# A graph network's edge scatter in groups of 8 columns instead of 16, with the last three tiles of layer 0 reordered

## The reference

```
h = relu(layernorm(x)); t1 = h @ W1
msg = t1[src] + (h[src] * h[dst]) @ W2, divided by sqrt(deg[src] * deg[dst])
e = leaky_relu(t1 + segment_sum(msg, dst) + b);  x = x + e / |e|
```

## Time and profile before

| | us |
|---|---|
| median of 3 runs (range) | 2204.69 (2198.97 to 2205.42) |
| the profiled execution | 2204.25 |
| its span, first to last instruction | 2202.4 |
| first and last scatter of GpSimd start at | 62.36, 1239.11 |
| layer 0's steps, first q to the last gather's end | 483.2 to 1313.5 |
| TensorE busy | 1871.7 (85%) |
| GpSimd busy | 1023.4 (46%) |
| mean granted TensorE clock | 0.895 |

### The profile page before, as it was taken

The page is one execution under the profiler, slowest core; times in us unless marked ns, Lnnn a source line. Parts: engine busy times, 40 slices in busy tenths (PEclk is TensorE's granted clock), DMA queues, the critical chain, the costliest instruction groups (busy, mean ns, idle before and its releaser), DMA issues. The chain is left out here.

```text
span 2202.4 us, 23568 instructions
## 1 busy us (share of the span) xinstructions
PE 1871.7 (85%) x7253; PEld 1153.6 (52%) x7253; DVE 1331.8 (60%) x1958; ACT 484.9 (22%) x635; POOL 1023.4 (46%) x1346
## 2 busy tenths in 40 slices
PE   5599768779999999755566699999879999999996
PEld 1178622257777777433345457777753444434442
DVE  6877678844444445422222355565458788878885
ACT  1000200025555555322233334200250000000000
POOL 1688777777888888888888400000005000000000
PEclk9755579889999999977778899999699999999998
DMA  7888860016666677433343441587016555656553
GB/s 269 328 328 328 336 226 9 9 61 240 239 239 239 243 243 254 157 120 120 140 159 131 167 142 63 192 283 242 27 42 171 155 158 167 189 163 179 166 164 102
DMA packets 338855, 395.86 MB, mean 180 GB/s; under 512 B 114026, under 2 KB 319572, under 8 KB 325843
## 3 DMA queue, kind: packets, MB, share of 16 engines
q1 hardware_dynamic: 219872, 307.83, 39.9%
q10 hardware_dynamic: 93110, 86.22, 11.9%
q0 software_dynamic: 25792, 0.87, 1.0%
HBM read 222.33 MB, written 172.51 MB: 179 GB/s over the span
## 5 line engine op out<-in xcount | busy, mean ns | idle before, releaser
L373 POOL DMA_INDIRECT table<-valT,idxT x806 | 815.9, 1012 | 251.5 <-issue 249.9
L1994 PE MATMUL psum<-wgt,big 128*65 128x384 f32 (+3 forms) x1600 | 527.7, 491 | 2.7 <-POOL big L1855 2.7
L1944 DVE SCALAR_TENSOR_TENSOR wgt<-ratio,l3q,fcj 128x768 f32<-128x768 f32 (+2 forms) x400 | 414.1, 1053 | 96.6 <-PE psum L1994 83.5
L1994 PEld LDWEIGHTS psum<-wgt,big 128*65 128x65 f32 x1600 | 219.0, 137 | 302.5 <-issue 296.0
L784 PE MATMUL psum<-hx,region 128*128 128x257 f32 x1250 | 299.2, 387 | 5.5 <-DVEq L572 5.0
L784 PE MATMUL psum<-region,g 128*128 128x512 f32 (+1 forms) x672 | 270.1, 547 | 1.0 <-DVE big L587 1.0
L587 DVE TENSOR_TENSOR big<-big,psum 128x512 f32<-128x512 f32 (+1 forms) x325 | 209.6, 664 | 86.8 <-PE psum L784 86.4
L784 PEld LDWEIGHTS psum<-hx,region 128*128 128x128 f32 x1250 | 233.6, 195 | 36.5 <-DVEq L572 5.4
L852 PE MATMUL psum<-ident,tk 128*128 128x128 f32 x625 | 104.8, 304 | 151.2 <-DMA tk<-table 150.7
L991 POOL PARTITION_ALL_REDUCE edges<-edge x1 | 0.5, 516 | 396.7 <-DVEq L1363 396.7
L784 PEld LDWEIGHTS psum<-region,g 128*128 128x128 f32 x672 | 121.9, 190 | 118.9 <-issue 112.8
(11 more groups left out here) (215 smaller groups left out, 1487.9 us busy)
## 6 DMA issues: line engine op xcount, KB each, us to landing
table<-tk SPq DMA_DIRECT2D x25, 3200.0 KB
fcj<-counts SPq DMA_DIRECT2D x150, 384.0 KB, 3.3
tk<-table SPq DMA_DIRECT2D x25, 1664.0 KB
counts<-region ACTq DMA_DIRECT2D x25, 1600.0 KB
tk<-table SPq DMA_DIRECT2D x25, 1536.0 KB
fcj<-counts SPq DMA_DIRECT2D x50, 448.0 KB, 3.6
counts_t<-region ACTq DMA_DIRECT2D x25, 800.0 KB
counts_b<-region ACTq DMA_DIRECT2D x25, 800.0 KB
```

Source lines behind the costliest of these rows:

```text
L373: eng.indirect_dma_start(out=table, out_offset=bass.IndirectOffsetOnAxis(idxT[:, c:c + 1], 0), in_=valT[:, c, :], in_offset=None, bounds_c ...
L1944: eng.scalar_tensor_tensor(out=wgt[:, n % NW, u, 0:w], in0=rb[:, 2 * i + u, t0 * P:t0 * P + w], scalar=qs[:, k, 2 * i + u:2 * i + u + 1], ...
L1994: last = eng.matmul(acc[p % 2][u][0:FW, b, 0:hi - lo], ftx[:, k, 2 * i + u, :], wgt[:, n % NW, u, lo:hi], start=k == 0, stop=k == NT - 1, ...
```

## The change

Groups have 8 columns, so there are 101, and 25 x 101 elements in the `within` operations (their buffer moves into a free part of `region`). The first 20 groups instead of 10 read `clr`. A group is reported when the seventh column of the next has been issued, as before; the last three when the third has been. The loop of `overlapped` is one turn shorter, and steps 21 to 24 stand written out: step 22 has no turn and no takes of tile 23 at its end (`more=False`), and step 23 (`ahead=True`) begins with all of prev = 22: the copy of wt, the diagonal, the 13 chunks of the gather and their lifts; only then come the turn and the takes of tile 23.

```diff
-GS = 16
-GR = 2
+GS = 8
+GR = 1
...
     step((0, 0, 0), None)
-    with eng.Fori(0, m - 1) as i:
+    with eng.Fori(0, m - 2) as i:
         step((2 * i + 1, 1, i), (2 * i, 0))
         step((2 * i + 2, 0, i + 1), (2 * i + 1, 1))
-    step((NT - 2, 1, m - 1), (NT - 3, 0))
+    step((NT - 4, 1, m - 2), (NT - 5, 0))
+    step((NT - 3, 0, m - 1), (NT - 4, 1), more=False)
+    step((NT - 2, 1, m - 1), (NT - 3, 0), ahead=True)
     step((NT - 1, 0, m), (NT - 2, 1), last=True)
     step(None, (NT - 1, 0))
...
-        within = buf("within", [1, 2, NT, NGS], BF16)
+        marks = region[0:1, :, :].rearrange("p a n -> p (a n)")[:, 6 * EC:6 * EC + NT * NGS].bitcast(BF16)
+        within = marks.rearrange("p (a n g) -> p a n g", a=2, n=NT)
...
-            late = 10
+            late = 20
...
-                    if g and c == min(EC, GS * g + 7) - 1:
+                    if g and c == GS * g + (6 if g < NGS - 3 else 2):
                         finish(g - 1)
...
                     itself(row(wt, prev[0]))
+                if ahead:
+                    for n in range(13):
+                        lift(n)
+                    own()
...
-                take(k, 3)
-                take(k, 4)
+                if not ahead:
+                    take(k, 3)
+                    take(k, 4)
                 if prev:
                     eng.wait_ge(sem("ag"), 13 * prev[0] + 1)
                     eng.activation(wt, tk[:, prev[1], :, :, 1], ACT.Copy).then_inc(sem("wt"), 1)
+                if ahead:
+                    for g in range(5):
+                        take(k, g)
...
+                if ahead:
+                    eng.wait_ge(sem("g1"), prev[0] + 1)
+                    eng.wait_ge(sem("diag"), prev[0] + 1)
+                    gathered(range(13))
+                    eng.wait_ge(sem(f"tk{cur[1]}0"), 16 * cur[2] + 16)
+                    for g in range(3):
+                        turn(cur[0], cur[1], g)
...
-                if not last:
+                if more and not last:
                     eng.wait_ge(sem(f"tk{1 - s}0"), 16 * (r + s) + 16)
                     for g in range(3):
                         turn(k + 1, 1 - s, g)
```

More of the change, by code:

```diff
@@ L575, in _, with step @@
             begun = ch.n
-            def step(cur, prev, last=False):
+            def step(cur, prev, last=False, more=True, ahead=False):
                 row = lambda t, k: t[:, bass.ds(k, 1), :].rearrange("p a d -> p (a d)")
@@ L620, in step @@
                     itself(tk[:, s, k, :, 1])
-                if prev:
+                if prev and not ahead:
                     for n in range(5 if last else 13):
                         lift(n)
-                if prev and not last:
+                if prev and not last and not ahead:
                     own()
@@ L774, in step @@
                     normal(k, hk)
-                else:
+                elif more:
                     for g in range(3):
@@ L853, in turn, with step, gathered @@
                 last.then_inc(sem("tc"), 1)
-            def step(cur, prev, last=False):
+            def step(cur, prev, last=False, more=True, ahead=False):
+                def gathered(chunks):
+                    j, z = prev
+                    of, g = (wt, g1) if cur else (tk[:, 0, :, :, 1], hk)
+                    for n in chunks:
+                        eng.wait_ge(sem("af"), 13 * j + max(n + 1, 3))
+                        if n < 12:
+                            mul = mm(pL[:, n % 3, :], g[:, n % 2 * P:n % 2 * P + P], of[:, 4 * (n // 2):4 * (n // 2) + 4, :], True, True)
+                        else:
+                            for o in range(2):
+                                mul = mm(pL[:, 0, o * P:o * P + P], g[:, o * P:o * P + P], of[:, NT - 1, :], True, True)
+                        mul.then_inc(sem("ag"), 1)
+                if ahead:
[5 more added lines that the diff above has]
+                        turn(cur[0], cur[1], g)
                 if cur:
@@ L869, in step @@
                     mul.then_inc(sem("q"), 1)
[L871 to L881, removed]
                 def turn_ab():
@@ L893, in dense @@
                     mul.then_inc(sem("e"), 1)
-                if prev:
+                between = prev and not ahead
+                if between:
                     eng.wait_ge(sem("g1"), prev[0] + 1)
```

## The result

The changed kernel took 2206.62 us (median of 22 runs, 2203.86 to 2211.14) against 2203.51 us of the kernel before on the same chip: ratio 1.0017, 95% interval 1.0011 to 1.0023. That is no difference by the bound of 0.3%, a loss of 2.4 to 5.1 us by the interval. I had forecast 2196.5 with a range of 2190 to 2203, so both the time and the range missed. The profiled execution took 2206.18 (span 2204.2), 1.9 more than that of before.

A forecast was written before the change was run, and what follows sets the result against it. Layer 0 was taken as bound by the scatter from tile 17 on; -4.4 (report) - 8.1 (tail) + 4.7 (pauses) = -7.8 from 2204.25 gave 2196.4, stated as 2196.5, range 2190 to 2203.

The forecast's parts named there:

- so 5.9 us more for the five: The five larger within operations on VectorE: 5.9 us longer, hidden by the long wait for tile 17 (36.2 us).
- Pauses, +4.7: GpSimd's waits every 112 columns of the scatter: loads moved against them lengthen it by 4.7 us, between 0 and 7.9.
- Tail, -8.1: Layer 0's end, tile 23 to tile 24: 7.5 us gained by moving tile 22's gather in front, plus 0.6 for TensorE's clock.
- The 0.6 for the clock: TensorE at tile 23: shorter idleness may save 0 to 1.2 us of lowered clock; half taken.
- the 3 to 5 forecast: TensorE before tile 23: the gather of tile 22 ends 3 to 5 us before tile 23 comes.
- Report, -4.4: Scatter's end: tile 23's last group is reported at column 802 instead of 805, 4.4 us sooner.
- The pauses take most of it: Second rival: scatter pauses grow by 7.6 us, gain 4.9, time 2199.5, no measurable difference; chance 0.3.
- Slower: Rival: each of 50 more reports holds GpSimd's queue 0.4 us, scatter ends 20 us later, time 2212; chance 0.07.
- a last column later than 1247: Sign in the changed trace: the scatter's last column, forecast at 1243.8, starting later than 1247 would mean no change.

The follow-up runs named there:

- the paced kernels: Before, changed kernel and variants with a second memset ahead of every column from 304 on: before 2521.52 us, changed 2520.83, changed with 112 rows 2514.89.

## Why the prediction was wrong

Two costs stood in the sum at nothing: the scatter's later start took 7.5 us, and the larger `within` operations took 3.85 us of GpSimd's time. A third term, the pauses, was sized at +4.7 and came to +0.5. Report and tail, which the reasoning was mostly about, came within 1.1 us of their 12.5. At layer 1's first matmul the account closes: +11.8 for the scatter's end, -4.6 - 7.5 + 0.8 = -11.4 behind it (rounded), so +0.4 where I had -7.8.

- *The start of the scatter*: it has no term in the sum. I took everything ahead of the one-hot loop as unchanged and did not list the load whose rows GR and NGS set. It cost 7.5 us in the trace; with 112 rows in the paced kernels column 0 came 5.9 us sooner, column 805 7.6, and the median fell by 5.9. This alone turns the forecast 2196.5 into no change.
- *"so 5.9 us more for the five. They stand in front of the one-hot loop ... That is covered"*: the size was right (12.57 us for 6.72), the cover was not. I asked who waits for VectorE's result and not who runs beside it. GpSimd lost 3.85 us in the trace and 2.3 in the paced kernels.
- *Pauses, +4.7*: the five from 337 on came to +0.5. Column 785 gave +0.4 for the +0.5 taken. The columns 337, 449 and 561, taken at +0.7 between -1.1 and +2.3, came to -2.9. Column 673 gave +3.0 for 3.5, but that its cause is the load, as I argued, is not shown: on the three slower chips its gap was 4.29 to 5.49 us in all six traces with groups of 16, too, and 3.36 in one with groups of 8. The pause at 113, which I left as it was, gave +0.9 of the +1.9 in 104 to 128. Its gap came out between 2.6 and 8.8 us in single executions, so a sum over the pauses of one trace carries several us of chance.
- *Tail, -8.1*: 7.5 measured, and 6.6 to 7.3 where the scatter is paced. From the end of q to tile 24's turn it took 4.79 us, forecast 5.3, before 12.75. The 0.6 for the clock did not come, 0.4 was lost: after 3.55 us of idleness the granted clock was 0.71 in 1251 to 1255 and 0.86 in 1255 to 1259, a part of each stretch at the lower level. Tile 23's twelve transposes took 2.30 us for 2.83, but the eight matmuls behind them 2.96 for 2.01. The gather ended 3.55 us before the tile, inside the 3 to 5 forecast. Right, and right for the reason given, that the wait covers it: where no tile is late the same edit costs 14.8 us.
- *Report, -4.4*: right. Tile 23's turn came 4.6 us nearer to column 805, and 6.3 in the paced kernels for 3 columns of 2.1.
- *The rivals.* "The pauses take most of it" forecast no measurable difference, and none came, but not by the pauses: its number was met by luck. "Slower" named reports that hold GpSimd's queue. It was not that: the columns from 128 to 805 took no longer with 101 reports than with 51 (978.0 us for 979.0). The sign that came true was the one I had named for no change, a last column later than 1247.
- *The arithmetic.* Two sums of the prediction don't add up: the second rival's pauses come to +6.9 and not +7.6 (1.6 + 3.5 + 1.8), and the low end of all pauses is -1.1 and not 0. Neither changes the outcome.

## What to carry to other kernels

When a diff changes a constant, list every instruction whose shape it sets, loads first: a row count that falls from 102 to 101 made a load nearly five times as long and cost about what the whole change was to gain. An operation off the chain still costs if an engine on the chain runs beside it, so for each added VectorE operation look at what GpSimd does in those microseconds; a trace of before with columns of 1.2 to 2.7 us among many of 0.97 shows it in advance. Work moved in front of a load pays while that load is late and costs as soon as it is not; know how late it is on every chip that the kernel must run on.

## What the runs showed of the hardware

- A load of 101 rows of 4096 B ran at 23 to 28 GB/s for 17.5 us, with at most two packets under way at once, and held up SP's next issue for 11.0 to 11.7 us and the other queue's loads; 102 rows took 3.7 us, and 112 left the start at 61.8 to 63.2 us.
- A column's indirect DMA on GpSimd took up to 3.00 us instead of 0.97 beside VectorE operations with two inputs from SBUF, even on one partition (1x2525), and ended 0.84 to 0.85 us behind their end; beside a reduce of the same size it took 0.97. A TENSOR_SCALAR of 128x806 held one to 1.23. The Trainium skill, "SBUF — State Buffer", in SBUF: two separate sides, has VectorE and GpSimd share a port pair, which an operation with two inputs in SBUF, or one in a mode that uses both ports, holds for its whole length. The rows with two inputs agree; no row tells the mode of the TENSOR_SCALAR.
- On three chips a hand-over from TensorE to VectorE took 7 us and more in some stretches of a loop, and before took 2286 to 2296 us instead of 2204.
- With three landing semaphores and one report in every 112 columns moved, the pauses of the scatter moved from every 112 columns to every 104, and those left fell to 1.7 us over a plain column.
